# Moving the decay products of chunk 3 and the cumulated sums within the scan of a hybrid kernel

## The reference

```python
x = x + conv_attention(group_norm(x))            # softmax attention over the 1024 points
t = tokens(x)                                    # 8 x 1024 tokens of 128
t = t + mamba(layer_norm(t))
t = t + experts(layer_norm(t))                   # 8 experts, top 2
...
# mamba
z, xBC, dt = split(rmsnorm(x) @ W_in.T)          # 256, 320, 8
xBC = silu(conv4(xBC) + conv_b)                  # causal, 4 taps; then xs 256, B 32, C 32
dt = softplus(dt + dt_bias);  dA = exp(dt * -exp(A_log))
state = state * dA_t + dt_t * x_t * B_t;  y_t = state . C_t      # over 1024 tokens, 8 heads
y = rmsnorm((y + D * xs) * silu(z)) ;  x + y @ W_out.T
```

## Time and profile before

| | us |
|---|---|
| runs | 954.06, 957.86, 958.05 (median 957.86) |
| profiled execution, its own time | 954.08 |
| its span, first to last instruction | 952.3 |
| busy in the span: PE / DVE / ACT / POOL | 858.4 / 724.0 / 503.3 / 290.8 |
| mean granted TensorE clock | 0.969 |

### The profile page before, as it was taken

How to read it: one execution, slowest core, us unless ns; L and a number is a source line. 1 busy time by engine, 2 the same in 40 slices (tenths; PEclk the granted TensorE clock), 3 DMA queues, 4 the chain that set the end, 5 groups by cost and what they waited for, 6 DMA issues and landing times.

```text
span 952.3 us, 18728 instructions
## 1 busy us (share of the span) xinstructions
PE 858.4 (90%) x7086; PEld 670.9 (70%) x7086; DVE 724.0 (76%) x1959; ACT 503.3 (53%) x740; POOL 290.8 (31%) x264
## 2 busy tenths in 40 slices
PE   3788999999998869898989899899789999999997
PEld 2555556656665758686868777776578898888887
DVE  2867677678767686868687787977968889888885
ACT  1524455455557457566575757464335544555453
POOL 0026110110010236354545454647530333033300
PEclk9979999999999879899999999999899999999999
DMA  5641011011100303213030303041000000000001
GB/s 150 192 143 23 1 23 23 1 23 23 23 1 0 77 4 74 48 31 71 8 76 3 78 1 78 1 96 50 2 1 1 24 23 24 1 23 23 24 2 44
DMA packets 30888, 36.07 MB, mean 38 GB/s; under 512 B 4560, under 2 KB 24912, under 8 KB 30800
## 3 DMA queue, kind: packets, MB, share of 16 engines
q1 hardware_dynamic: 29648, 30.68, 13.2%
q10 hardware_dynamic: 1152, 4.19, 1.2%
HBM read 21.50 MB, written 4.98 MB: 28 GB/s over the span
## 4 chain that ended last, share of the span: by engine, by line
PE 58%; DVE 27%; ACT 7%; issue 5%; POOL 2%; SPq 0%; DMA 0%; DVEq 0%; POOLq 0%; ACTq 0%
PE ps L1047 7%; PE ps L715 6%; DVE cacc L1713 5%; DVE acc L1997 5%; PE ps L702 4%; PE ps L794 3%; PE ps L969 3%; PE ps L796 3%; PE ps L669 3%; PE ps L795 3%; PE ps L674 2%; PE ps L691 2%; PE ps L905 2%; PE ps L684 2%; PE ps L919 2%
## 5 line engine op out<-in xcount | busy, mean ns | idle before, releaser
L1997 DVE SCALAR_TENSOR_TENSOR acc<-ps,comb,acc 128x128 f32<-128x128 f32 x512 | 139.8, 343 | 16.2 <-PE ps L1047 15.6
L1400 ACT ACTIVATE hid<-ps,b_f 128x512 f32<-128x512 f32 x128 | 87.2, 687 | 112.2 <-PE ps L796 112.1
L1047 PEld LDWEIGHTS ps<-w_f,hid 128*128 128x128 f32 x1024 | 130.6, 191 | 19.5 <-ACT hid L1400 8.0
L1047 PE MATMUL ps<-w_f,hid 128*128 128x128 f32 x1024 | 136.8, 277 | 5.0 <-ACT hid L1400 4.5
L1570 DVE TENSOR_REDUCE nmax<-ps 128x1 f32<-128x1024 f32 x64 | 78.1, 1220 | 29.7 <-PE ps L674 29.4
L1713 DVE SCALAR_TENSOR_TENSOR cacc<-ps,cw,cacc 128x1023 f32<-128x1023 f32 (+5 forms) x72 | 91.8, 1275 | 9.4 <-ACT cacc L1272 7.7
L1341 ACT ACTIVATE dcy<-ps 128x1024 f32<-128x1024 f32 x64 | 65.2, 1018 | 62.4 <-PE ps L919 62.3
L570 POOL TENSOR_TENSOR srs<-sve,neg_half 128x1 f32<-128x1 f32 x64 | 58.4, 912 | 117.7 <-DVE gram L1822 117.6
L1187 ACT ACTIVATE probs<-ps,nmax 128x1024 f32<-128x1024 f32 x64 | 71.3, 1113 | 39.2 <-DVE nmax L1570 36.5
L1805 DVE SCALAR_TENSOR_TENSOR dcy<-dcy,g_sb 128x1024 f32<-128x1024 f32 x64 | 85.4, 1334 | 0.3
L702 PEld LDWEIGHTS ps<-id_f,probs 128*128 128x128 f32 x512 | 59.0, 142 | 33.0 <-issue 23.3
(11 more groups left out here) (214 smaller groups left out, 1865.3 us busy)
## 6 DMA issues: line engine op xcount, KB each, us to landing
c_dec<-exp_dram SPq DMA_DIRECT2D x32, 256.0 KB, 5.4
xc<-in_x SPq DMA_DIRECT2D x8, 512.0 KB, 3.6
q_b<-q_a SPq DMA_DIRECT2D x16, 256.0 KB, 2.8
X<-in_x_tok ACTq DMA_DIRECT2D x8, 512.0 KB, 5.3
c_rep<-cacc SPq DMA_DIRECT2D x32, 128.0 KB, 4.6
out<-o_ch SPq DMA_DIRECT2D x8, 512.0 KB, 2.6
w_f<-in_w SPq DMA_DIRECT2D x2, 512.0 KB, 4.1
cst_f<-in_sel_rows SPq DMA_DIRECT2D x1, 512.0 KB, 4.4
```

What stands on the lines that cost most here:

```text
L1047: last = nc.tensor.matmul(ps[:, Y_BANKS[n], t * P:(t + 1) * P], hid[n % 2][:, t * P:(t + 1) * P], w2_f[:, e, :], start=True, stop=True)
L1400: nc.scalar.activation(hid[n % 2][:], ps[:, 4 + n % 2, :], ACT.Gelu, bias=b1_f[:, n // 2:n // 2 + 1]).then_inc(e_hidden_ready, 1)
L1997: done = nc.vector.scalar_tensor_tensor(acc[u][:, tt, :], ps[:, bank, t * P:(t + 1) * P], comb[u][:, tt, e:e + 1], acc[u][:, tt, :], ALU.m ...
```

## The change

TensorE and ScalarE issue the decay product and the exponential of the chunk three further on at chunk 0 (chunk 1 in block 0), TensorE behind the increments and ScalarE ahead of the silu block, and skip them in the next chunk. The cumulated sums go from slot 6.5 to slot 7, ScalarE's factors from 7 to 7.5. On VectorE the exponents go from 7 to 7.5, the third tap of group 1 from 6 to 5, the first tap of group 2 from 7 to 6, the second from -0.25 of the next block to 7, and the third from 0 to -0.25.

```diff
@@ PE
             def scan(b, u, first, last):
                 for c in range(NT):
                     n = NT * b + c
-                    if n + 2 < NT * B:
+                    if n + 2 < NT * B and c != (2 if first else 1):
                         decay(n + 2)
...
                         increments(b, u)
+                    if c == (1 if first else 0):
+                        decay(n + 3)
                     pieces(b, c + 0.5)
...
-                        (group, (1, 1), 2, 4.5), (group, (2, 0), 2, 5.5), (group, (2, 1), 2, 5.5), (cumulate, (), 2, 6.5)]
+                        (group, (1, 1), 2, 4.5), (group, (2, 0), 2, 5.5), (group, (2, 1), 2, 5.5), (cumulate, (), 2, 7)]
@@ ACT
-                    if NT * b + c + 2 < NT * B:
+                    if NT * b + c + 2 < NT * B and c != (2 if first else 1):
                         decays(NT * b + c + 2)
+                    if c == (1 if first else 0):
+                        decays(NT * b + c + 3)
                     if first and c == 1:
                         factors(1, 1)
                     pieces(b, c)
...
-                         (shortcut, (4, NT), 1, 5.5), (factors, (), 2, 7)]
+                         (shortcut, (4, NT), 1, 5.5), (factors, (), 2, 7.5)]
@@ DVE
-            dve_parts = [("conv", (2, 2), 1, -0.25), ("conv", (2, 3), 1, 0), ("ends", (), 1, 1), ("low", (), 2, 2.75),
+            dve_parts = [("conv", (2, 3), 1, -0.25), ("ends", (), 1, 1), ("low", (), 2, 2.75),
                          ("inner", (), 1, 3), ("conv", (0, 1), 2, 4), ("conv", (0, 2), 2, 4), ("conv", (0, 3), 2, 4),
-                         ("steps", (), 2, 4.5), ("conv", (1, 1), 2, 5), ("conv", (1, 2), 2, 5),
-                         ("softplus", (0,), 2, 5.5), ("softplus", (1,), 2, 5.5), ("conv", (1, 3), 2, 6),
-                         ("exponents", (), 2, 7), ("conv", (2, 1), 2, 7)]
+                         ("steps", (), 2, 4.5), ("conv", (1, 1), 2, 5), ("conv", (1, 2), 2, 5), ("conv", (1, 3), 2, 5),
+                         ("softplus", (0,), 2, 5.5), ("softplus", (1,), 2, 5.5), ("conv", (2, 1), 2, 6),
+                         ("conv", (2, 2), 2, 7), ("exponents", (), 2, 7.5)]
```

## The result

| | before | after |
|---|---|---|
| median of 4 runs each on the same chip | 956.75 | 1016.72 (1014.99 to 1017.53) |
| ratio to before, with its 95% interval | | 1.0628 [1.0599, 1.0658] |
| profiled execution, its own time | 954.08 | 1017.53 |
| its span | 952.3 | 1015.7 |
| mean granted TensorE clock | 0.969 | 0.937 |

The changed kernel is 60 us slower; the forecast was 1001, with a range of 974 to 1018. All engines do the same work as before, but TensorE's takes longer. This is the page's busy line of TensorE after the change; before, the same 7086 instructions took 858.4 us.

What follows compares the result with a forecast made beforehand. TensorE, 90% busy, was taken as the bound, with ScalarE's and VectorE's chains close beside it. Chains +32.5 us and clock +14.5 us gave +47.0 on 954.08: 1001 us, range 974 to 1018.

Steps and rivals of the forecast that it cites:

- ScalarE's chain, +4.0: First half of a steady block: ScalarE idles for chunk 3's exponential, so the group product comes 4.0 us later.
- VectorE's chain, +2.1: End of a steady block: exponents stand behind two taps and chunk 7's gating, so the gates come 2.1 us later.
- So ScalarE's chain sets the time: Ahead of the group product: TensorE is ready 2 us before the mask, so ScalarE's chain decides.
- The wait for the mask: TensorE's wait ahead of the group product, 0.34 us before, was to grow to 2 us.
- The clock, 2.41 us at six gates: Low clock after the gates' wait in blocks 1 to 6, 2.41 us each, +14.5 us in all.
- the clock falls twice a block: Rival: a second fall after the group product's wait, another 2 us for each of six blocks, 1013 us; chance 0.13.
- the 2.13 us waits of blocks 3 to 5: TensorE's waits ahead of the cumulated sums; the clock stayed at 1.00, held against a second fall.
- Block 0, +6.1: Block 0 has both moves one chunk later and nearly the same chains, so it loses 6.1 us.
- Block 6 and behind: Block 6: only the transposes late, +1.3 us, plus 2.41 us for the clock; block 7: nothing.
- +47.0 us: Whole forecast loss, the chains' 32.5 us and the clock's 14.5 us, on the profiled execution's 954.08 us.
- +32.5 us at an unchanged clock: Both chains' loss without the clock: blocks 1 to 5 +25.1, block 0 +6.1, block 6 +1.3 us.

Runs made afterwards that it cites:

- The half alone: Only chunk 3's decay product and exponential moved, against the kernel before: 992.33 us (985.98 to 998.5), ratio 1.0385.
- the run with all waits filled: Changed kernel plus unread products ahead of the gates (6), x transposes (4) and normed tokens' transposes (6): 1000.34 us, 1.0448 to the kernel before.

## Why the prediction came out as it did

**ScalarE's chain, +4.0: right.** The silu block's exponential starts 6.63 us into the block for 5.46 in the forecast, and 1.17 of that is the clock behind the gates (the increments' end at 5.86 for 4.69). With that added, the forecast has the token norms at 15.3, `xh` at 21.2 and the mask's end at 26.6; the trace has 15.04, 21.29 and 26.56. The half alone gave 3.9 a block.

**VectorE's chain, +2.1: right.** From the group product to the gates 25.14 us for the forecast's 25.0, with a wait of 3.36 us at the gates where 3.4 was said, behind the taps that were named.

**"So ScalarE's chain sets the time", TensorE 2 us ahead: wrong.** This step failed. It took the token norms' end as what releases the transposes of the normed tokens. They wait for the first gather of x as well, which on ScalarE stands behind the norms and the exponential of chunk 4. TensorE waits 2.77 us there, its clock falls, and the stretch to the group product takes 9.35 us for 6.2. The gather by itself only ate the lead of 2 us: the transposes start 20.18 us into the block, and 6.2 on top of that is 26.4, about the mask's end at 26.56. The 3 us that were lost are the clock's. In the run with all waits filled the group product waits for the mask again, 0.33 us (at 587.67). The mask that the forecast let TensorE wait for is ready 3 us before TensorE comes. A reader of the earlier trace rows had no wait at L831 to see, since the gather was early enough in the kernel before; it stands in the code only. The wait for the mask, forecast as growing to 2 us, fell to nothing.

**The clock, 2.41 us at six gates: mis-sized, in both directions.** In a steady block the fall behind the gates costs 1.17 us up to the decay product, half of the charge. The charge was read in block 1, and in block 1 of the changed kernel too it is higher, 1.9 us (407.29 to 413.88, less 4.69). The fall at the inner products, charged with nothing, costs 3.0 more. Together the falls cost 4.5 us a block, 54.67 less the 50.15 of the filled block at full clock. The rival "the clock falls twice a block" is what happened, with its second fall earlier than it was put (inner products, not group product), at 1013 us against 1016.7. The forecast held the 2.13 us waits of blocks 3 to 5 as the reason against it.

**Block 0, +6.1: too little.** It lost 12.6 us, 1.3 of it before the chunks that were moved. Its first half lost 9.4 of these (42.73 us between the decay products at 345.20 and 387.93, for 33.35 from 343.91 to 377.26 before), with the inner products at 3.75 us: the same fall as in the other blocks, charged here with none. Block 6 and behind: 4.1 us for 3.7 with the clock's charge.

**The sum and the range.** The forecast's +47.0 us is 16.4 short of the 63.4 between the two traces: 9.5 in blocks 1 to 5, 6.5 in block 0, 0.4 behind. What the forecast calls "+32.5 us at an unchanged clock" is a sum at full clock, for it counts blocks 1 to 5 from the 226.9 us that the falls in the kernel before had already lengthened by 5.2. The measured 1016.7 us lies 1.3 us below the top of the range. That top was set by the rival with a second fall at the group product, at 2 us each, and by 3.8 us for the scatter of the runs; the second fall that came costs 3.0 and lies elsewhere. That the range holds is in part luck.

The Trainium skill, page "TensorE: Matmul & The Clock Gate", section "HAM oscillation", speaks of a loop with a wait in every turn that restarts cold in each. The trace after agrees: two falls in each of blocks 1 to 5 (0.71 and 0.63 in the block shown). The trace before has a wait in every turn too, 2.13 us in each of blocks 3 to 5, and stays at 1.00; but the waits of the page's loop are longer than that.

What stays open: why a wait of one length is followed by the low clock in one block and not in the next. The runs show that it is so, and that filling waits or moving them shifts it; none shows what decides. The order of the instructions alone does not: block 0 has the same instructions in the changed kernel and in the three that fill its waits (at the gates, at the normed tokens' transposes, at all three), since the filling begins in block 1; its inner products took 3.75, 2.02, 2.85 and 3.75 us. The Trainium skill, same page, section "Part 1: The HAM clock gate", says that the gate looks at TensorE's activity by a rhythm that runs free of the program, so that one kernel comes out differently from run to run. That would fit block 0 and the scatter of the first half alone (985.98 to 998.5 us), but no run here shows the rhythm.

## What to carry to other kernels

When a piece is moved later on one engine, list every semaphore that its consumers wait for, those that never ended a wait in the old trace too, for one of them may end the new one, as the gather did here. Count the time that a wait costs twice on TensorE: the wait, and the slow products that may follow it, which matter only where TensorE has no time in hand. Where a run hits its expected number, look whether the blocks of its trace do too: three runs here hit or nearly hit theirs by another way. A short wait in every block can be worth filling with products that nobody reads, if the filler needs no later semaphore than the wait it fills.

## What was not expected of the hardware

- Waits of nearly one length, 1.83 to 1.85 us at the x transposes, were followed by the low clock in some blocks (transposes 3.56 and 3.28 us) and not in others (1.97). The 2.15 us wait of the kernel before was followed by it in block 1 and not in blocks 3 to 5.
- The clock also fell with no wait right ahead, behind the step products: at 468.53 in the kernel before, and in three of five blocks of the run with all waits filled. There, ahead of the fall at 540.25, TensorE's last wait, 0.33 us, had ended at 535.92.
- Unread products lowered the time, by up to 16 us in the changed kernel and 0.4% in the kernel before, though TensorE had more to do.
